# Linear attention with tokens on partitions: the divisor beside the sums, one reciprocal of 128x4, and quotients turned by TensorE

## The chip, the core and the metric
One NeuronCore of a Trainium2 chip runs the whole program in one launch. The metric is the device time of that launch in microseconds. Its engines are TensorE (PE in the profile; its weight loads are PEld), VectorE (DVE), ScalarE (ACT), GpSimd (POOL) and SyncE (SP, which here only issues DMAs). They run side by side and meet at semaphores. Matmuls read SBUF and write PSUM; PSUM has banks of 128 partitions by 512 fp32.

## The reference
All tensors are fp32. Input x is 2 x 1024 x 512. A block of causal linear attention (16 heads of 128, 4 heads of keys and values, so 4 query heads share one of each) is followed by a feed-forward block with 2-of-4 sparsity; both have a LayerNorm before and behind them and are added to x. What concerns us:

```python
q, k = rope(q), rope(k)                     # 128 per head
qf, kf = elu(q) + 1.0, elu(k) + 1.0
def step(carry, inp):                       # over 1024 tokens
    state = state + k_s[..., :, None] * v_s[..., None, :]
    z = z + k_s
    num = jnp.einsum('bhe,bhed->bhd', q_s, state)
    den = jnp.einsum('bhe,bhe->bh', q_s, z)[..., None] + 1e-06
    return ((state, z), num / den)
return out @ Wo.T                           # then layernorm, + x
# afterwards: h = silu(x @ w_gate) * (x @ w_up); of each 4 the 2 largest |h| stay; h @ w_down
```

## The kernel before
The scan is done in chunks of 128 tokens. Each operand of a matmul is split into a high part (fp32r) and a low part (the rest), and a product is three matmuls: high x high, low x high, high x low (the helper `three`, L450).

The attention is 64 slots: 8 units (2 batches by 4 key heads) of 8 chunks, one unit having 4 query heads. Function `slot_a(s)` exists once for each engine and issues what that engine does in slot s; the order in which these functions are written is the order of each engine's queue. Three chunks are in flight: slot s computes scores for chunk s, sums for chunk m = s - 1 and the output projection for chunk s - 2.

- Scores (L564): keys x queries of 4 heads, 128 x 512, into `bank_s`. The vector engine multiplies by the causal mask (L982), ScalarE rounds to `s_hi` (L773), GpSimd subtracts to get `s_lo` (L1159, helper `lo`).
- Sums (L536 to L542), features of v on partitions: the numerator of 4 heads, 128 x 512, in `psO`, from v and the scores and from the running state `st_hi`, `st_lo` and the queries. The divisor has a bank of its own, `psD`: ones x scores, and a state column of k's sum spread over 128 columns. It is the same on all 128 partitions. Both together are `bank_od`.
- State (L548 to L552): keys x values with a column of ones, 128 x 130, accumulated in `bank_st` over 7 chunks; ScalarE and the vector engine take it apart in two steps each (L760, L761, L975, L976).
- Quotient: ScalarE takes the logarithm of the divisor (L764) and exp of its negative (L769) as a first 1/d; the vector engine improves it with L991 and L997 and multiplies with the numerator in L1002. This reads `bank_od` until its end, and the next slot's sums wait for it (`dve_a`). ScalarE rounds the quotient to `a_hi` (L787), GpSimd makes `a_lo`.
- Output (L578): 12 matmuls of quotient by wout into `bank_y`, added into `y_acc` (L1013).

Among them each slot has a projection of queries for a later chunk (12 matmuls of 512 columns, `queries`), and every fourth slot one of keys, one of values, and turns of these and of x (4 transposes each, L497, L504, L476). In slots with odd s the vector engine starts with the rotation of the new queries (L913 to L922), which can begin when they are projected. Every job of normalisation (L887) waits for a small power step on GpSimd (L1166). In the feed-forward half (`slot_f`) all is projection and selection.

Of the kernel before, what the change touches and what calls it, by code (L numbers as in the profile page):

```python
# [7 lines left out]
ALU = mybir.AluOpType  # L8
ACT = mybir.ActivationFunctionType
# [156 lines left out]
def build(nc, x, wq, wk, wv, wo, wg, wu, wd, cos_t, sin_t, causal, eye, x1, out):  # L166
    with ExitStack() as ctx:
# [26 lines left out]
        Sth = sb("st_hi", [P, 2, P], F32R)  # L194
        Stl = sb("st_lo", [P, 2, P], F32R)
# [5 lines left out]
        small = sb("small", [P, 48])  # L201
# [11 lines left out]
        shift = [small[:, 40 + i:41 + i] for i in range(4)]  # L213

# [4 lines left out]
        rotk, xk, Ek, Sf, r0, Tn = [scr[:, i, :] for i in range(10, 16)]  # L219
# [42 lines left out]
        def sums(m):  # L262
            if m >= FREE and m % 2 == 0:
                return psQ[:, 0, :], psQ[:, 1, :]
            return psO, psD
# [40 lines left out]
        act_sth, act_ln, act_r0, act_sh, act_ah = [sem(n) for n in ("act_sth", "act_ln", "act_r0", "act_sh", "act_ah")]  # L306
# [3 lines left out]
        dve_T, dve_U, dve_a, dve_y = sem("dve_T"), sem("dve_U"), sem("dve_a"), sem("dve_y")  # L310
        pool_fl, pool_kl, pool_sl, pool_al = sem("pool_fl"), sem("pool_kl"), sem("pool_sl"), sem("pool_al")
# [135 lines left out]
        def _(pe):  # L447
# [67 lines left out]
            def slot_a(s):  # L515
# [4 lines left out]
                if 0 <= m < SLOTS:  # L520
# [3 lines left out]
                    psM, psN = sums(m)  # L524
                    o3 = psM.rearrange("p (h t) -> p h t", h=4)
                    d3 = psN.rearrange("p (h t) -> p h t", h=4)
                    qh, ql = big_h[:, p % 2, :, t], big_l[:, p % 2, :, t]
# [8 lines left out]
                    three(psM, Vh[:, c, 0:P], Vl[:, c, :], Sh[:, :], Sl[:, :], True, first)  # L536
                    pe.matmul(psN, ones[:, :], Sh[:, :], start=True, stop=False, skip_group_check=True)
                    ins = pe.matmul(psN, ones[:, :], Sl[:, :], start=False, stop=first, skip_group_check=True)
                    if not first:
                        g.wait_ge(dve_stl, 7 * u + ms)  # L540
                        three(o3, Sth[:, 0, :], Stl[:, 0, :], qh, ql, False, True)
                        ins = three(d3, Sth[:, 1, :], Stl[:, 1, :], qh, ql, False, True)  # L542
                    ins.then_inc(pe_pv, 1)
                    if ms < 7:
# [5 lines left out]
                        pe.matmul(psSt[:, 0:VP], KTl[:, c, :], Vh[:, c, :], start=False, stop=False,  # L550
                                  skip_group_check=True)
                        pe.matmul(psSt[:, 0:P], KTh[:, c, :], Vl[:, c, :], start=False, stop=True,  # L552
# [5 lines left out]
                if 0 <= s < SLOTS:  # L558
# [4 lines left out]
                    g.wait_ge(dve_s, s)  # L563
# [9 lines left out]
                if 0 <= m2 < SLOTS:  # L573
                    g.wait_ge(pool_al, m2 + 1)
# [4 lines left out]
                    ins.then_inc(pe_y, 1)  # L579

# [19 lines left out]
            def slot_f(n):  # L600
                tick = tick_f(n)
                if n < SLOTS:
# [7 lines left out]
                    if n > 0:  # L610
                        g.wait_ge(dve_s, SLOTS)
# [54 lines left out]
        def _(act):  # L666
# [77 lines left out]
            def slot_a(s):  # L744
# [11 lines left out]
                if 0 <= m < SLOTS:  # L756
                    u, ms = m // 8, m % 8
                    if ms < 7:
                        g.wait_ge(pe_st, 7 * u + ms + 1)
                        copy(Sth[:, 0, :], psSt[:, 0:P])  # L760
                        copy(Sth[:, 1, :], psSt[:, P:P + 1].to_broadcast([P, P])).then_inc(act_sth, 1)  # L761
                    g.wait_ge(pe_pv, m + 1)
                    g.wait_ge(dve_U, m)
                    act.activation(r0, sums(m)[1], ACT.Ln, bias=eps_den[:, 0:1]).then_inc(act_ln, 1)  # L764
                if s % 4 == 0 and 0 < s < SLOTS:
                    values_split(s // 4)
                if 0 <= m < SLOTS:
                    g.wait_ge(act_ln, m + 1)
                    act.activation(r0, r0, ACT.Exp, scale=-1.0).then_inc(act_r0, 1)  # L769
# [14 lines left out]
                if 0 <= m < SLOTS:  # L784
                    g.wait_ge(dve_a, m + 1)
# [76 lines left out]
        def _(dve):  # L862
# [94 lines left out]
            def slot_a(s):  # L957
# [56 lines left out]
                if s % 4 == 0 and 0 < s < SLOTS:  # L1014
                    turned_low(s // 4)
# [293 lines left out]
```

## Time and profile before

| | us |
|---|---|
| median of 3 runs | 1312.8 (1311.62 to 1313.56) |
| profiled execution, its own time | 1309.38 |
| its span | 1307.6 |
| PE busy | 1245.6 (95%) |
| DVE busy | 935.0 (72%) |
| POOL busy | 675.9 (52%) |
| ACT busy | 570.7 (44%) |

Times in the rows are microseconds from the span's start; the profiled execution took 1.8 us more than its span. An engine's busy time counts from the start of its instructions to their ends. TensorE's matmuls overlap, each starting before the one before has ended, so the rate is read from start to start. The attention takes the time up to about 757 us.

### The profile page before, as it was taken

The numbers are of one execution on the slowest core, as the hardware profiler recorded it, in microseconds if no ns is written. First come the engines' busy times: TensorE is split into PE (matmuls) and PEld (weight loads), VectorE is DVE, ScalarE is ACT, GpSimd is POOL, SyncE is SP. The second block draws the span as 40 slices with busy tenths as digits, with TensorE's granted clock in tenths as the row PEclk, the third lists the DMA queues.
The fourth block names the chain that finished last, engine by engine and source line by source line (L and its number), as shares of the span: only waits on it lengthen the run. The fifth ranks groups of instructions, "written<-read, shape, count | busy, mean of one in ns | idle before, by whom it ended". The sixth has DMA issues, their size and how long they took to land.

```text
span 1307.6 us, 15436 instructions
## 1 busy us (share of the span) xinstructions
PE 1245.6 (95%) x5543; PEld 1008.7 (77%) x5543; DVE 935.0 (72%) x1426; ACT 570.7 (44%) x1002; POOL 675.9 (52%) x524
## 2 busy tenths in 40 slices
PE   7889999999998899999998899999999999999996
PEld 7668778888787687787786677888888878888885
DVE  8678778878777777887867746666657775555568
ACT  4544654655554555546455433333333233332322
POOL 6365665565567756655646754343434644242414
PEclk9899999999999999999999999999999999999998
DMA  5321312211322312222212232222122321121103
GB/s 185 101 57 49 91 55 57 65 57 33 97 81 73 105 49 77 69 57 81 56 25 75 92 101 64 65 60 62 42 64 65 121 73 57 41 57 41 49 1 112
DMA packets 50347, 90.26 MB, mean 69 GB/s; under 512 B 6496, under 2 KB 6752, under 8 KB 50272
## 3 DMA queue, kind: packets, MB, share of 16 engines
q1 hardware_dynamic: 50272, 89.29, 23.1%
q8 instruction: 44, 0.72, 0.2%
q14 instruction: 31, 0.25, 0.1%
HBM read 64.09 MB, written 8.39 MB: 55 GB/s over the span
## 4 chain that ended last, share of the span: by engine, by line
PE 63%; DVE 17%; POOL 8%; ACT 5%; issue 4%; DMA 2%; SPq 1%; DVEq 0%; POOLq 0%
PE bank_q L451 6%; PE bank_q L453 6%; PE bank_q L452 6%; PE bank_od L451 6%; PE bank_od L453 6%; PE bank_od L452 6%; PE bank_t L451 3%; PE bank_t L452 3%; PE bank_t L453 3%; POOL s_lo L1159 3%; PE bank_s L451 3%; PE bank_s L453 3%; PE bank_s L452 3%; PE bank_y L451 2%; PE bank_y L453 2%
## 5 line engine op out<-in xcount | busy, mean ns | idle before, releaser
L1159 POOL TENSOR_TENSOR big_lo<-scratch,big_hi 128x1024 fp32r<-128x1024 f32 (+1 forms) x64 | 150.4, 2360 | 236.1 <-ACT big_hi L817 217.1
L1159 POOL TENSOR_TENSOR w_lo<-stage,w_hi 128x512 fp32r<-128x512 f32 x96 | 153.3, 1605 | 68.3 <-ACT w_hi L701 66.8
L451 PE MATMUL bank_q<-x_hi,w_hi 128*128 128x512 f32 x440 | 173.0, 393 | 1.3 <-DVE scratch L917 1.3
L453 PE MATMUL bank_q<-x_lo,w_hi 128*128 128x512 f32 x440 | 171.9, 391 | 0.0
L452 PE MATMUL bank_q<-x_hi,w_lo 128*128 128x512 f32 x440 | 171.6, 390 | 0.0
L1159 POOL TENSOR_TENSOR s_lo<-scratch,s_hi 128x512 fp32r<-128x512 f32 x64 | 94.5, 1477 | 140.7 <-ACT s_hi L773 140.7
L808 ACT ACTIVATE scratch<-scratch 128x512 f32<-128x512 f32 x64 | 40.5, 632 | 233.4 <-DVE scratch L1076 233.2
L1159 POOL TENSOR_TENSOR a_lo<-scratch,a_hi 128x512 fp32r<-128x512 f32 x64 | 82.9, 1295 | 97.2 <-ACT a_hi L787 97.2
L451 PE MATMUL bank_y<-wout_hi,a_hi 128*128 128x512 f32 x256 | 103.2, 403 | 6.1 <-POOL a_lo L1159 3.0
L787 ACT CAST a_hi<-scratch 128x512 fp32r<-128x512 f32 x64 | 39.7, 621 | 155.6 <-DVE scratch L1002 155.6
L1094 DVE TENSOR_TENSOR y_acc<-bank_od,y_acc 128x512 f32<-128x512 f32 x44 | 30.2, 686 | 101.5 <-PE bank_od L453 101.5
L453 PE MATMUL bank_y<-wout_lo,a_hi 128*128 128x512 f32 x256 | 101.3, 396 | 0.0
L452 PE MATMUL bank_y<-wout_hi,a_lo 128*128 128x512 f32 x256 | 101.3, 396 | 0.0
L451 PEld LDWEIGHTS bank_q<-x_hi,w_hi 128*128 128x128 f32 x440 | 82.8, 188 | 19.0 <-issue 1.7
L452 PEld LDWEIGHTS bank_q<-x_hi,w_lo 128*128 128x128 f32 x440 | 82.7, 188 | 17.6
L453 PEld LDWEIGHTS bank_q<-x_lo,w_hi 128*128 128x128 f32 x440 | 82.6, 188 | 17.7
L927 DVE SCALAR_TENSOR_TENSOR scratch<-scratch 128x1024 f32<-128x1024 f32 x31 | 42.9, 1383 | 48.6 <-ACT scratch L736 48.6
L451 PE MATMUL bank_t<-x_hi,w_hi 128*128 128x512 f32 x192 | 76.0, 396 | 1.6 <-DVE kt_lo L949 1.4
L817 ACT CAST big_hi<-scratch 128x512 fp32r<-128x512 f32 x64 | 39.2, 623 | 86.6 <-DVE scratch L1048 76.2
L452 PE MATMUL bank_t<-x_hi,w_lo 128*128 128x512 f32 x192 | 75.7, 394 | 0.0
L453 PE MATMUL bank_t<-x_lo,w_hi 128*128 128x512 f32 x192 | 75.6, 394 | 0.0
L773 ACT CAST s_hi<-scratch 128x512 fp32r<-128x512 f32 x64 | 39.8, 622 | 70.2 <-DVE scratch L982 70.2
(285 smaller groups left out, 3436.9 us busy)
## 6 DMA issues: line engine op xcount, KB each, us to landing
scratch<-scratch SPq DMA_DIRECT2D x124, 128.0 KB, 2.6
x_rows<-x SPq DMA_DIRECT2D x56, 256.0 KB, 2.9
stage<-wq SPq DMA_DIRECT2D x32, 256.0 KB, 2.7
stage<-wo SPq DMA_DIRECT2D x32, 256.0 KB, 2.6
stage<-wg SPq DMA_DIRECT2D x32, 256.0 KB, 2.7
stage<-wu SPq DMA_DIRECT2D x32, 256.0 KB, 2.6
stage<-wd SPq DMA_DIRECT2D x32, 256.0 KB, 2.6
x<-x_rows SPq DMA_DIRECT2D x16, 256.0 KB, 2.3
```

The lines of the kernel that those rows point to most:

```text
L451: pe.matmul(ps, whi, xhi, start=first, stop=False, skip_group_check=True)
L452: pe.matmul(ps, wlo, xhi, start=False, stop=False, skip_group_check=True)
L453: return pe.matmul(ps, whi, xlo, start=False, stop=last, skip_group_check=True)
L773: copy(Sh[:, :], Sf).then_inc(act_sh, 1)
L787: copy(Ah[:, :, :].rearrange("p h t -> p (h t)"), Tn).then_inc(act_ah, 1)
L808: act.activation(ab[:, i, :], hid[:, i, :], ACT.Abs).then_inc(act_ab, 1)
L817: copy(big_h[:, d % 2, i, :], hid[:, i, :]).then_inc(act_hh, 1)
L927: dve.scalar_tensor_tensor(whole, grown, 1.0, whole, ALU.min, ALU.add).then_inc(dve_f, 1)
L1094: dve.tensor_tensor(Y[:, t, :], down_bank(y), Y[:, t, :], ALU.add).then_inc(dve_yf, 1)
L1159: return pool.tensor_tensor(dst, full, hi.bitcast(F32), ALU.subtract)
```

## The change
The sums are formed with tokens on partitions. The scores of a head (128 x 128) are now the weights, and v with its column of ones (130 columns) is streamed; the same with queries and the state. So a head's sums are 130 columns wide, and column 128 is its divisor, one value for each token, which is a partition. Four heads lie in two banks (`sums(m)[:, h // 2, h % 2, :]`). The divisor's bank, the ones and the spread state column go. Division is then: 4 divisors out of PSUM with the offset, one reciprocal of 128 x 4, one multiplication with a broadcast operand, all on the vector engine. The output projection needs features on partitions, so TensorE turns the 4 quotients by transposes into `bank_s`, which the mask has read by then; ScalarE rounds from there, and the low part is made by the vector engine instead of GpSimd. The scores of the next chunk now wait for that low part (`dve_al`). The state is taken out in one step by each of ScalarE and the vector engine.

```diff
         def sums(m):
-            if m >= FREE and m % 2 == 0:
-                return psQ[:, 0, :], psQ[:, 1, :]
-            return psO, psD
+            both = psQ if m >= FREE and m % 2 == 0 else psOD
+            return both[:, :, 0:2 * VP].rearrange("p g (i d) -> p g i d", i=2)
...
@@ TensorE, slot_a
-                    three(psM, Vh[:, c, 0:P], Vl[:, c, :], Sh[:, :], Sl[:, :], True, first)
-                    pe.matmul(psN, ones[:, :], Sh[:, :], start=True, stop=False, skip_group_check=True)
-                    ins = pe.matmul(psN, ones[:, :], Sl[:, :], start=False, stop=first, skip_group_check=True)
                     if not first:
                         g.wait_ge(dve_stl, 7 * u + ms)
-                        three(o3, Sth[:, 0, :], Stl[:, 0, :], qh, ql, False, True)
-                        ins = three(d3, Sth[:, 1, :], Stl[:, 1, :], qh, ql, False, True)
+                    for h in range(4):
+                        o = sums(m)[:, h // 2, h % 2, :]
+                        sh, sl = Sh[:, h * P:(h + 1) * P], Sl[:, h * P:(h + 1) * P]
+                        qh, ql = big_h[:, p % 2, h, t], big_l[:, p % 2, h, t]
+                        pe.matmul(o, sh, Vh[:, c, :], start=True, stop=False, skip_group_check=True)
+                        pe.matmul(o[:, 0:P], sh, Vl[:, c, :], start=False, stop=False, skip_group_check=True)
+                        ins = pe.matmul(o, sl, Vh[:, c, :], start=False, stop=first, skip_group_check=True)
+                        if not first:
+                            pe.matmul(o, qh, Sth[:, :], start=False, stop=False, skip_group_check=True)
+                            pe.matmul(o, qh, Stl[:, :], start=False, stop=False, skip_group_check=True)
+                            ins = pe.matmul(o, ql, Sth[:, :], start=False, stop=True, skip_group_check=True)
...
                     g.wait_ge(pool_fl, 2 * p + 2)
-                    g.wait_ge(dve_s, s)
+                    g.wait_ge(dve_al, s - 1)
...
                 if 0 <= m2 < SLOTS:
-                    g.wait_ge(pool_al, m2 + 1)
+                    g.wait_ge(dve_al, m2 + 1)
...
+                if 0 <= m < SLOTS:
+                    g.wait_ge(dve_a, m + 1)
+                    g.wait_ge(dve_s, min(s + 1, SLOTS))
+                    for h in range(4):
+                        ins = pe.transpose(psS[:, h * P:(h + 1) * P], Tn[:, h * P:(h + 1) * P], ident[:, :])
+                    ins.then_inc(pe_at, 1)
@@ ScalarE, slot_a
                     if ms < 7:
+                        g.wait_ge(pe_pv, m)
                         g.wait_ge(pe_st, 7 * u + ms + 1)
-                        copy(Sth[:, 0, :], psSt[:, 0:P])
-                        copy(Sth[:, 1, :], psSt[:, P:P + 1].to_broadcast([P, P])).then_inc(act_sth, 1)
-                    g.wait_ge(pe_pv, m + 1)
-                    g.wait_ge(dve_U, m)
-                    act.activation(r0, sums(m)[1], ACT.Ln, bias=eps_den[:, 0:1]).then_inc(act_ln, 1)
+                        copy(Sth[:, :], psSt[:, 0:VP]).then_inc(act_sth, 1)
...
-                    act.activation(r0, r0, ACT.Exp, scale=-1.0).then_inc(act_r0, 1)
...
-                    g.wait_ge(dve_a, m + 1)
+                    g.wait_ge(pe_at, m + 1)
                     g.wait_ge(pe_y, m)
-                    copy(Ah[:, :, :].rearrange("p h t -> p (h t)"), Tn).then_inc(act_ah, 1)
+                    copy(Ah[:, :, :].rearrange("p h t -> p (h t)"), psS[:, :]).then_inc(act_ah, 1)
@@ VectorE, slot_a
-                    dve.scalar_tensor_tensor(Tn, sums(m)[1], EPS_DEN, r0, ALU.add, ALU.mult).then_inc(dve_T, 1)
+                    g.wait_ge(pe_pv, m + 1)
+                    dve.tensor_scalar(den.rearrange("p (g i o) -> p g i o", g=2, i=2), sums(m)[:, :, :, P:P + 1],
+                                      EPS_DEN, None, ALU.add).then_inc(dve_den, 1)
+                    g.wait_ge(dve_den, m + 1)
+                    dve.reciprocal(share, den).then_inc(dve_share, 1)
+                    g.wait_ge(dve_share, m + 1)
+                    g.wait_ge(pe_at, m)
+                    dve.tensor_tensor(Tn.rearrange("p (g i d) -> p g i d", g=2, i=2), sums(m)[:, :, :, 0:P],
+                                      share.rearrange("p (g i o) -> p g i o", g=2, i=2).to_broadcast([P, 2, 2, P]),
+                                      ALU.mult).then_inc(dve_a, 1)
...
-                    dve.scalar_tensor_tensor(Tn, Tn, 2.0, r0, ALU.subtract, ALU.mult).then_inc(dve_U, 1)
...
-                    dve.scalar_tensor_tensor(Tn, Tn, -1.0, sums(m)[0], ALU.mult, ALU.mult).then_inc(dve_a, 1)
...
+                if 0 <= m < SLOTS:
+                    g.wait_ge(act_ah, m + 1)
+                    g.wait_ge(pe_y, m)
+                    dve.tensor_tensor(Al[:, :, :].rearrange("p h t -> p (h t)"), psS[:, :],
+                                      Ah[:, :, :].rearrange("p h t -> p (h t)").bitcast(F32),
+                                      ALU.subtract).then_inc(dve_al, 1)
@@ GpSimd, slot_a
-                if 0 <= m < SLOTS:
-                    g.wait_ge(act_ah, m + 1)
-                    lo(Al[:, :, :].rearrange("p h t -> p (h t)"), Tn,
-                       Ah[:, :, :].rearrange("p h t -> p (h t)")).then_inc(pool_al, 1)
```

The vector engine's queue in slot s = 9 (m = 8, the first chunk of a unit), before, from the rotation's last step to the output's addition:

```order
L922 TENSOR_TENSOR scratch<-scratch 128x1024
L894 TENSOR_TENSOR x_lo<-bank_t,x_hi 128x4x128
L975 TENSOR_TENSOR st_lo<-bank_st,st_hi 128x128
L976 TENSOR_TENSOR st_lo<-bank_st,st_hi 128x128
L982 TENSOR_TENSOR scratch<-bank_s,mask 128x512
L991 SCALAR_TENSOR_TENSOR scratch<-bank_od,scratch 128x512
L997 SCALAR_TENSOR_TENSOR scratch<-scratch 128x512
L1002 SCALAR_TENSOR_TENSOR scratch<-scratch,bank_od 128x512
L1011 COPY y_acc<-bank_y 128x512
```

The same place in the changed kernel (its own line numbers):

```order
L926 TENSOR_TENSOR scratch<-scratch 128x1024
L898 TENSOR_TENSOR x_lo<-bank_t,x_hi 128x4x128
L979 TENSOR_TENSOR st_lo<-bank_st,st_hi 128x130
L985 TENSOR_TENSOR scratch<-bank_s,mask 128x512
L993 TENSOR_SCALAR small<-bank_od 128x4
L996 RECIPROCAL small<-small 128x4
L999 TENSOR_TENSOR scratch<-bank_od,small 128x512
L1015 COPY y_acc<-bank_y 128x512
L1021 TENSOR_TENSOR a_lo<-bank_s,a_hi 128x512
```

The product (L999) stands right behind the two small steps, ahead of any normalising step of the slot, and the low part of the quotients is new at the end.

TensorE's queue in the same slot of the changed kernel, from the last head's sums to the next projection of queries; before, 5 matmuls of 512 columns stood for the 12 small ones and nothing stood between the output and the queries:

```order
L539 MATMUL bank_od<-v_hi,s_hi 128x130
L540 MATMUL bank_od<-v_lo,s_hi 128x128
L541 MATMUL bank_od<-v_hi,s_lo 128x130
L551 MATMUL bank_st<-v_hi,kt_hi 128x130
L553 MATMUL bank_st<-v_lo,kt_hi 128x128
L555 MATMUL bank_st<-v_hi,kt_lo 128x130
L452 MATMUL bank_s<-big_hi,k_hi 128x512
L453 MATMUL bank_s<-big_hi,k_lo 128x512
L454 MATMUL bank_s<-big_lo,k_hi 128x512
...
L454 MATMUL bank_y<-wout_lo,a_hi 128x512
L588 MATMUL bank_s<-ident,scratch 128x128 x4
L452 MATMUL bank_q<-x_hi,w_hi 128x512
```

The transposes (L588) come between the output and the queries, so whatever they wait for, the projections behind them wait for too.

## Rows read from the trace of the kernel before

**Rows 1.** The page: busy time of each engine, share of the span, instructions.

```profile
PE 1245.6 (95%) x5543; PEld 1008.7 (77%) x5543; DVE 935.0 (72%) x1426; ACT 570.7 (44%) x1002; POOL 675.9 (52%) x524
```

**Rows 2.** Busy us by stretch: PE, PEld, DVE, ACT, POOL, granted clock, DMA.

```profile
64.00:696.00 632.00, 605.80 (x2733) 488.12 (x2733) 493.62 (x705) 338.09 (x600) 379.22 (x266) 0.99 0.23 65
696.00:757.00 61.00, 49.95 (x213) 36.79 (x213) 44.55 (x72) 29.56 (x58) 41.84 (x38) 1.00 0.26 81
...
406.30:409.70 3.40, 3.28 (x8) 2.63 (x9) 2.29 (x4) 3.03 (x4) 1.57 (x2) 0.50 0.05 18
```

**Rows 3.** Waits of TensorE: us in total, times, longest us.

```profile
PE bank_od L451 <- DVE scratch L1002: 21.1, 16, 3.1
...
PE bank_od L451 <- POOL s_lo L1159: 5.4, 4, 2.4
...
PE bank_q L451 <- POOL s_lo L1159: 2.5, 3, 1.1
```

**Rows 4.** Timeline of TensorE, slot m = 8: start us, duration us, what.

```profile
148.99 0.40 PE L538 MATMUL bank_od<-s_lo,ones 128*128 128x512 f32 x1
149.23 0.22 PE L548 MATMUL bank_st<-v_hi,kt_hi 128*128 128x130 f32 x1
149.29 0.28 PE L550 MATMUL bank_st<-v_hi,kt_lo 128*128 128x130 f32 x1
149.40 0.27 PE L552 MATMUL bank_st<-v_lo,kt_hi 128*128 128x128 f32 x1
149.51 0.45 PE L451 MATMUL bank_s<-big_hi,k_hi 128*128 128x512 f32 x1
149.80 0.40 PE L452 MATMUL bank_s<-big_hi,k_lo 128*128 128x512 f32 x1
```

**Rows 5.** Timeline of TensorE, four transposes of values.

```profile
410.54 0.60 PE L497 MATMUL bank_t<-ident,scratch 128*128 128x128 f32 x4
410.90 0.47 PE L451 MATMUL bank_s<-big_hi,k_hi 128*128 128x512 f32 x1
411.21 0.39 PE L452 MATMUL bank_s<-big_hi,k_lo 128*128 128x512 f32 x1
```

**Rows 6.** Timeline, slot m = 8: the vector engine's chain, TensorE's first query matmul.

```profile
147.65 1.22 DVE L913 TENSOR_TENSOR scratch<-bank_q,scratch 128x1024 f32<-128x1024 f32 x1
...
150.10 2.28 DVE L922 TENSOR_TENSOR scratch<-scratch 128x1024 f32<-128x1024 f32 x1
...
153.30 0.67 DVE L982 TENSOR_TENSOR scratch<-bank_s,mask 128x512 f32<-128x512 f32 x1
...
153.06 0.39 PE L451 MATMUL bank_q<-x_hi,w_hi 128*128 128x512 f32 x1
```

**Rows 7.** Groups of instructions: busy us, mean ns; one line: ns min/median/max.

```profile
L975 DVE TENSOR_TENSOR st_lo<-bank_st,st_hi 128x128 fp32r<-128x128 f32 x56 | 15.8, 282 | 6.8 <-ACT st_hi L761 6.6
...
L881 DVE BATCH_NORM_AGGREGATE small<-small 128x2 f32<-128x6 f32 x64 | 11.6, 182 | 2.2
...
L1159 POOL TENSOR_TENSOR a_lo<-scratch,a_hi 128x512 fp32r<-128x512 f32 x64 | 82.9, 1295 | 97.2 <-ACT a_hi L787 97.2
...
L922 DVE TENSOR_TENSOR scratch<-scratch x31: 1249/1957/2525, 29.0 to 691.0; 128x1024 f32<-128x1024 f32 x31
```

**Rows 8.** Timeline of the first slots: mask of m = 0, sums of m = 1.

```profile
66.88 0.67 DVE L982 TENSOR_TENSOR scratch<-bank_s,mask 128x512 f32<-128x512 f32 x1
...
70.06 0.50 PE L451 MATMUL bank_od<-s_hi,v_hi 128*128 128x512 f32 x1 [2.41 <-POOL s_lo L1159]
```

**Rows 9.** Timeline of ScalarE: the logarithms of m = 58 and m = 62.

```profile
712.70 0.71 ACT L764 ACTIVATE scratch<-bank_q,small 128x512 f32<-128x512 f32 x1
...
747.59 0.70 ACT L764 ACTIVATE scratch<-bank_q,small 128x512 f32<-128x512 f32 x1
```

**Rows 10.** Timeline of TensorE at the start: streams of 128-column matmuls.

```profile
2.67 5.38 PE L639 MATMUL bank_t<-ones 128*128 128x128 f32 x24 [2.67 <-DVE v_hi L1112]
...
11.89 1.53 PE L639 MATMUL bank_t<-ones 128*128 128x128 f32 x12
```

**Rows 11.** Weight loads of line 538: busy us, mean ns.

```profile
L538 PEld LDWEIGHTS bank_od<-s_lo,ones 128*128 128x128 f32 x61 | 11.9, 195 | 2.9
```

More of the change, by code:

```diff
@@ L193, in build @@
         Al = sb("a_lo", [P, 4, P], F32R)
-        Sth = sb("st_hi", [P, 2, P], F32R)
-        Stl = sb("st_lo", [P, 2, P], F32R)
+        Sth = sb("st_hi", [P, VP], F32R)
+        Stl = sb("st_lo", [P, VP], F32R)
         ones = sb("ones", [P, P], F32R)
@@ L200, in build @@
         xr = sb("x_rows", [P, RING_R, W])
-        small = sb("small", [P, 48])
+        small = sb("small", [P, 52])
         Wh = [w_hi[:, i, :] for i in range(6)] + [Kh[:, :], Sh[:, :]]
@@ L213, in build @@
         shift = [small[:, 40 + i:41 + i] for i in range(4)]
+        den, share = small[:, 44:48], small[:, 48:52]
         M1, M2, xq = scr[:, 0:2, :], scr[:, 2:4, :], scr[:, 4:6, :]
@@ L218, in build @@
         sinb = scr[:, 8:10, :]
-        rotk, xk, Ek, Sf, r0, Tn = [scr[:, i, :] for i in range(10, 16)]
+        rotk, xk, Ek, Sf, zero, Tn = [scr[:, i, :] for i in range(10, 16)]
         vT = rotk
@@ L305, in build @@
         act_qe, act_qh = sem("act_qe"), sem("act_qh")
-        act_sth, act_ln, act_r0, act_sh, act_ah = [sem(n) for n in ("act_sth", "act_ln", "act_r0", "act_sh", "act_ah")]
+        pe_at = sem("pe_at")
+        act_sth, act_sh, act_ah = sem("act_sth"), sem("act_sh"), sem("act_ah")
         dve_q, dve_x, dve_f = sem("dve_q"), sem("dve_x"), sem("dve_f")
@@ L309, in build @@
         dve_stl, dve_s, dve_vl, dve_ktl = sem("dve_stl"), sem("dve_s"), sem("dve_vl"), sem("dve_ktl")
-        dve_T, dve_U, dve_a, dve_y = sem("dve_T"), sem("dve_U"), sem("dve_a"), sem("dve_y")
-        pool_fl, pool_kl, pool_sl, pool_al = sem("pool_fl"), sem("pool_kl"), sem("pool_sl"), sem("pool_al")
+        dve_den, dve_share, dve_a, dve_al, dve_y = [sem(n) for n in ("dve_den", "dve_share", "dve_a", "dve_al", "dve_y")]
+        pool_fl, pool_kl, pool_sl = sem("pool_fl"), sem("pool_kl"), sem("pool_sl")
         pe_g, pe_u, pe_d = sem("pe_g"), sem("pe_u"), sem("pe_d")
@@ L523, in slot_a @@
                     first = ms == 0
[L524 to L527, printed above, removed]
                     g.wait_ge(pool_sl, m + 1)
@@ L549, in slot_a @@
                                   skip_group_check=True)
-                        pe.matmul(psSt[:, 0:VP], KTl[:, c, :], Vh[:, c, :], start=False, stop=False,
+                        pe.matmul(psSt[:, 0:P], KTh[:, c, :], Vl[:, c, :], start=False, stop=False,
                                   skip_group_check=True)
-                        pe.matmul(psSt[:, 0:P], KTh[:, c, :], Vl[:, c, :], start=False, stop=True,
+                        pe.matmul(psSt[:, 0:VP], KTl[:, c, :], Vh[:, c, :], start=False, stop=True,
                                   skip_group_check=True).then_inc(pe_st, 1)
@@ L610, in slot_f @@
                     if n > 0:
-                        g.wait_ge(dve_s, SLOTS)
+                        g.wait_ge(dve_al, SLOTS)
                     project(psG[n % 2], j, half).then_inc(pe_g, 1)
@@ L974, in slot_a @@
                     g.wait_ge(act_sth, i + 1)
[L975 to L977 removed]
+                    dve.tensor_tensor(Stl[:, :], psSt[:, 0:VP], Sth[:, :].bitcast(F32),
+                                      ALU.subtract).then_inc(dve_stl, 1)
                 if 0 <= s < SLOTS:
@@ L1107, in _ @@
             dve.memset(Sf, 1.0).then_inc(dve_const, 1)
-            dve.memset(r0, 0.0).then_inc(dve_const, 1)
+            dve.memset(zero, 0.0).then_inc(dve_const, 1)
             g.wait_ge(dve_const, 2)
@@ L1112, in _ @@
             dve.tensor_copy(Vh[:, :, P + 1:P + 2],
[L1113 removed]
+                            zero[:, 0:4].rearrange("p (c o) -> p c o", o=1)).then_inc(const_ok, 1)
             variance(FIRST[0])
```

12 lines of the change are left out of this document (removed).

## The prediction, on record before the change was run

> **What bounds the kernel now.** I read the busy shares first [rows 1]: the reader is to see TensorE at 95% and no other engine above 72%. Then the two stretches of the attention half [rows 2]: in 64 to 696 us TensorE is busy for 606 of 632 us, in its last 61 us only for 50; the feed-forward half behind them (757 to 1307 us, 550 us) is not touched by the change. Third, who TensorE waits for [rows 3]: nearly all of it stands before the first matmul of the sums, for the last vector step of the slot before (L1002) or for s_lo from GpSimd. So the change pays in two currencies: what TensorE has to issue per slot, and what it waits for in a slot. A slot is one pass of slot_a, 64 of them; m is the slot whose sums are formed, 8 slots make a unit, and "first" slots are those with m a multiple of 8.
>
> Busy times of matmuls overlap, so I count start to start. A 512-column matmul takes 0.23 us (148.99 to 149.23), one of 128 or 130 columns with its own weights 0.11 (149.29, 149.40, 149.51), and the step from the small ones back to wide ones costs 0.06 more in the second wide one (149.51 to 149.80 is 0.29) and is given back by the short first one (149.23 to 149.29) [rows 4]. Four transposes and what follows: 410.54 to 410.90, then 0.31 instead of 0.23, together 0.44 us [rows 5].
>
> **Sums and state on TensorE: +8.1 us.** In an ordinary slot, 11 wide matmuls and 3 small ones now take 11 x 0.233 + 0.34 = 2.90 us; afterwards 24 + 3 small ones take 27 x 0.112 = 3.02. That is +0.12 in 56 slots, 6.7 us. In the 8 first slots 5 wide ones (and 3 small) become 12 small ones: 15 x 0.112 = 1.68 for 1.50, +1.4 us. Moving 512 columns as four times 128 saves no time here, because each piece brings its own weight load; the saving of the change is that the divisor rides along.
>
> The trace has 0.11 us for a small matmul with its load. The Trainium skill ("TensorE: Matmul & The Clock Gate", section "Back-to-back issue gap") gives about 81 ns for such a pair of 128 columns in a stream; by it, 1720 new small matmuls would cost 53 us less. The trace does not agree in either place where it has such pairs, and the same page's load time of columns over 1.2 (107 ns for 128, section "LDWEIGHTS") fits the rows.
>
> **Transposes: +28.2 us.** 64 x 0.44 us; nothing covers them, they stand on the engine that bounds.
>
> **What TensorE no longer waits for.** The sums of a slot wait for L1002 because it reads their banks, and L1002 stands behind a logarithm, an exponential, two more vector steps and the normalising step, which itself waits for GpSimd. Afterwards the banks are free one short chain after the mask: offset, reciprocal, product. The 16 waits for L1002 are 21.1 us in the view; it counts from the modelled end of the matmul before, 0.17 us after the next could start (0.40 long, 0.23 pitch), so they are 23.8. The 7 waits for s_lo are 7.9 + 1.2 = 9.1 [rows 3]. The first of these (2.6, at 70.06 [rows 8]) and the 5.5 us of the last slots are counted below. Left are 24.8 us, and I take all of them as gone: s_lo follows the mask by 2 us, the wait for the product comes sooner and stops TensorE first. With them goes 0.08 us of exposed weight load in 16 places, 1.3 us, and some 1 us of waits for wout_lo, whose queue on GpSimd gets shorter. Four of the waits were followed by a clock of 1.2 GHz for 3.4 us (granted 0.50, the last of the four is in rows 2), at most 1.7 us lost in each, in sum 6.3 us by the pitch of 0.43 there. Sum: -33.4 us.
>
> **The last slots: -10 us.** Without projections of queries TensorE needs some 6.55 us a slot, but the logarithms of m = 58 and 62 start at 712.70 and 747.59 [rows 9], 8.7 us a slot. They are held by the ring mask, s_hi, s_lo (1.3 to 1.7 us, behind a_lo, w_lo and an addition), deviation, normalise, L1002, a_hi, a_lo. The change takes a_lo from GpSimd and the normalising step out of the way of the banks. After the mask's end at M I get s_lo at M+2.0, the deviation at M+3.3, normalise M+3.9, Y added M+4.5, the new low part M+5.2, and the next scores want it at about M+5.5. So TensorE bounds, at 7.1 us a slot: 4 x 2.2 idle us go, and 1.7 at the last Y; 0.5 stays.
>
> **The wait that is added: +9.8 us.** The transposes need the product, which needs the mask, and queued behind them on TensorE are the queries, keys and values, and so everything. The vector engine's new chain after the mask is two small steps and one of 512. Neither small step is in the trace. Nearest is the aggregate on 6 columns, 0.18 us; above it a 128-column step from PSUM, 0.28 [rows 7]; below, nothing. I take 0.18 each (the widths are 4), 0.04 between dependent steps, 0.68 for the product (the mask has the same shape and a broadcast operand), together 1.13 us. At 0.28 each the late slots add 5 us, at nothing they give back 6.
> Slot m = 8 shows it [rows 6]. Rotation starts at 147.65, when the queries end; the mask ends at 153.97, the product would at 155.1; but Y has ended by 153.06, 2.0 us before. What helps: L922 took 2.28 there because GpSimd ran big_lo beside it (the line's fastest is 1.25 [rows 7]), and with a_lo gone big_lo runs earlier; one small step less before the mask (0.2). TensorE takes 0.2 more. That leaves 0.9 us. It holds for the first slots, whose sums are short: 8 x 0.9. Slot m = 32 has a variance before its rotation and I give it 2.1. In the others rotation or the keys' turn also end late now (mask 2.3 us late in m = 9 and its like), but from the transposes of the slot before, TensorE needs 12.0 us (24 projections at 0.23 and 6.5 for the rest), as the key projection lies between, and I read some 11 for the other engines. In m = 3, 7, ... the mask comes at once and 0.1 to 0.3 us is left. For these together 1.5 us.
>
> **The start: +3.0 us.** In m = 0 the mask starts at 66.88 [rows 8], so the transposes at 68.8; the queries that ran before it now follow, and the next sums begin near 71.8 instead of 70.06: +1.7. TensorE then stands for 5 us, and I put 1.3 us of slow clock behind it.
>
> **Covered, at nothing.** ScalarE loses the logarithm, the exponential and half of st_hi, GpSimd 1.3 us a slot [rows 7], and the vector engine three steps of 512 and a small one for the product, the low part of 0.68 and the two small ones, about 1 us net; all were idle for 20% or more. The low part on the vector engine stands behind normalise, but the next scores that wait for it come 6 us after the transposes. If that cover goes it costs what normalise is late; the longest wait for L1002 was 3.1 us [rows 3].
>
> **Sum.** 8.1 + 28.2 - 33.4 - 10 + 9.8 + 3.0 = +5.7 us on the profiled execution's 1309.4 (span 1307.6): 1315.1. The median of the runs lies 3.4 higher, so 1318.5.
>
> **Rivals.**
> - The wait at the transposes does not come, and neither do its slots' others: DVE and GpSimd gain so much that product and Y always meet. Then 9.8 and the start's 3.0 fall away: 1306, faster by 7. For it speaks that GpSimd's load falls by 12% (82.9 of 675.9 us) [rows 1, 7] and L922 varies from 1.25 to 2.5 with it; against it the 2.0 us of m = 8, a chain whose start TensorE itself sets.
> - The wait comes in full. The comparison of m = 8 made for all slots, with the engines as they run now, leaves 50 us of shortfall instead of 9.8, of which the 8 first slots have 16 and m = 9, 17, ... as much. Some 24 us of it would come back as work of the others overlapping: 1318.5 + 16 to 40, middle 1343. For it: the vector engine is 78% busy here [rows 2] and TensorE has given its slack away in the middle of the slot; against: after a stall it starts its next chain relatively earlier.
> - Small matmuls run at 0.081 us. As said above, 1720 x 0.031 = 53 us less, 1265. Both groups of rows speak against it.
> - The load is left out where two matmuls in a row have the same weights (2 of 6 in a head, 1 of 3 in the state). Each would save half of 0.112: 9 of them in 56 slots and 5 in 8, 544 x 0.056 = 30 us less, 1288. Against it: L538 loads the ones again right behind L537 [rows 11].
> - The clock. With 31 small steps in a slot TensorE might be given 1.2 GHz once per slot; a slow stretch costs 1.7 us [rows 2], 64 of them 109 us, 1427. Against it: at the start the pitch halved, from 0.22 to about 0.11, in a stream of nothing but 128-column matmuls and transposes [rows 10]. The Trainium skill (same page, "PE-mode transpose") says that transposes do not count as activity; by that, this rival is likelier than I have it, but the four that the trace has in every fourth slot have brought no fall.
>
> **How the numbers follow.** Forecast 0.52, own range 1310 to 1328 (the unknown small steps 11 us wide, the start and the last slots 3 each); no wait 0.24; wait in full 0.15; the last three 0.03 each. A change within 0.2% (2.6 us) can't be told from none. Faster: nearly all of the second case, the fourth and third, and a little of the first, 0.28. Same 0.17, from the low part of the first and the top of the second. Slower 0.55. The range goes from 1300 to 1342: below it lie the two cases of cheap matmuls, above it the clock and the upper half of the wait in full.
>
> **What the profile after would show.** Right: small matmuls at 0.11 pitch; no wait for the product before the sums; waits of TensorE before the transposes, on the vector engine, about 1 us in the first slots; TensorE's instruction count up, 64 x 4 transposes at 0.44; the last slots 7 us apart; few stretches at 0.50. Wrong: waits before the transposes in most slots, or before the scores for the low part; an offset or reciprocal well over 0.2 us; a pitch under 0.1; a clock that falls in each slot.

## The result, and the profile after

| | median us | runs | profiled execution us | span us | granted clock |
|---|---|---|---|---|---|
| before | 1311.5 | 20 (1309.31 to 1315.15) | 1309.38 | 1307.6 | 0.989 |
| changed | 1313.85 | 20 (1312.74 to 1314.91) | 1313.69 | 1311.9 | 0.991 |

The changed kernel is slower by 2.35 us, ratio 1.0016 [1.0009, 1.0022]: the direction of the forecast (+5.7 us, to 1318.5), less than half its size, and under the 0.2% that I had set as the bound of "no change". Note that the two profiled executions are 4.3 us apart and the medians 2.35. One run of the kernel before, in the chip's slow state (1528 us at a granted clock of 0.753), is left out of every figure here.

The page of the changed kernel, busy time of each engine:

```profile
PE 1271.0 (97%) x6583; PEld 1072.6 (82%) x6583; DVE 889.3 (68%) x1434; ACT 486.7 (37%) x818; POOL 561.4 (43%) x460
```

Against [rows 1] TensorE issues 1040 matmuls more; every other engine got lighter, GpSimd by 114 us. Still the time rose: what TensorE has to issue counted for more.

The same stretches as [rows 2]; the last two rows are the two stretches with a slow clock behind the first transposes and in slot m = 32:

```profile
64.00:696.00 632.00, 620.22 (x3587) 535.14 (x3588) 448.54 (x700) 260.35 (x431) 272.98 (x208) 0.99 0.24 64
696.00:757.00 61.00, 58.05 (x365) 50.44 (x362) 40.46 (x77) 23.08 (x43) 33.21 (x31) 1.00 0.31 91
...
67.50:73.90 6.40, 5.47 (x15) 4.50 (x16) 2.32 (x5) 2.28 (x4) 1.47 (x2) 0.50 0.62 164
432.60:435.40 2.80, 2.80 (x8) 2.21 (x7) 1.74 (x3) 1.67 (x3) 0.57 (x2) 0.50 0.82 229
```

TensorE's 26 idle us in the long stretch are 12 now, its 11 idle us in the last are 3. The waits of TensorE, to be read beside [rows 3] (us in total, times, longest):

```profile
PE bank_s L588 <- DVE scratch L999: 14.3, 11, 4.8
PE bank_s L477 <- DVE x_lo L898: 6.5, 1, 6.5
PE bank_od L452 <- DVE y_acc L1104: 2.7, 1, 2.7
```

The 29.0 us of waits for L1002 and s_lo are gone without a rest. A new wait stands at the transposes (L588) for the product (L999): 4.8 us in m = 0, the remaining ten together 9.5. The other two rows are not of the change.

TensorE in slot m = 8, small matmuls and then the step to wide ones (compare [rows 4]):

```profile
152.71 0.27 PE L539 MATMUL bank_od<-v_hi,s_hi 128*128 128x130 f32 x1
152.82 0.27 PE L540 MATMUL bank_od<-v_lo,s_hi 128*128 128x128 f32 x1
152.93 0.28 PE L541 MATMUL bank_od<-v_hi,s_lo 128*128 128x130 f32 x1
153.04 0.28 PE L551 MATMUL bank_st<-v_hi,kt_hi 128*128 128x130 f32 x1
...
156.69 0.40 PE L454 MATMUL bank_y<-wout_lo,a_hi 128*128 128x512 f32 x1
157.66 0.66 PE L588 MATMUL bank_s<-ident,scratch 128*128 128x128 f32 x4 [0.56 <-DVE scratch L999]
158.07 0.48 PE L452 MATMUL bank_q<-x_hi,w_hi 128*128 128x512 f32 x1
```

The pitch (the step from one start to the next) is 0.11 us. From 152.71 (L539) to 152.82 (L540) the weights are the same, s_hi, and the step is 0.11 like any other: no load is left out. From the last matmul of Y (the output projection) to the transposes it is 0.97, so 0.74 of waiting. The vector engine in front of it (compare [rows 6]):

```profile
153.97 1.23 DVE L926 TENSOR_TENSOR scratch<-scratch 128x1024 f32<-128x1024 f32 x1
...
155.92 0.68 DVE L985 TENSOR_TENSOR scratch<-bank_s,mask 128x512 f32<-128x512 f32 x1
156.52 0.15 DVE L993 TENSOR_SCALAR small<-bank_od 128x4 f32<-128x4 f32 x1
156.70 0.18 DVE L996 RECIPROCAL small<-small 128x4 f32<-128x4 f32 x1
156.91 0.69 DVE L999 TENSOR_TENSOR scratch<-bank_od,small 128x512 f32<-128x512 f32 x1
```

From the mask's end to the product's end is 1.00 us; 1.13 had been forecast.

Groups of instructions (busy us, mean ns; for [rows 7]):

```profile
L1021 DVE TENSOR_TENSOR a_lo<-bank_s,a_hi 128x512 fp32r<-128x512 f32 x64 | 43.8, 684 | 14.8 <-ACT a_hi L791 14.8
...
L999 DVE TENSOR_TENSOR scratch<-bank_od,small 128x512 f32<-128x512 f32 x61 | 42.2, 691 | 2.3 <-DVE small L996 0.3
...
L926 DVE TENSOR_TENSOR scratch<-scratch 128x1024 f32<-128x1024 f32 x31 | 39.8, 1284 | 1.1
...
L996 DVE RECIPROCAL small<-small 128x4 f32<-128x4 f32 x64 | 11.4, 178 | 2.2
L993 DVE TENSOR_SCALAR small<-bank_od 128x4 f32<-128x4 f32 x61 | 9.1, 150 | 0.0
```

**A budget of TensorE.** For each kernel I split the time from the first instruction to the first down-projection matmul by the steps from one matmul's start to the next. A step up to 0.26 us is issue. Of a longer one 0.23 is issue, and what is over that is put down by the step's length to an exposed load (up to 0.38; a weight load that the matmul before did not cover), to the slow clock (up to 0.45) or to a wait (beyond). The bounds are mine: a small matmul at half clock, 0.22 us, still counts as issue.

| us | end | waits | slow clock | exposed | issue |
|---|---|---|---|---|---|
| before | 794.2 | 52.8 | 8.3 | 11.8 | 721.2 |
| changed | 798.2 | 26.6 | 4.5 | 10.2 | 757.0 |
| measured | +4.0 | -26.2 | -3.8 | -1.6 | +35.8 |
| forecast | +5.7 | -24.3 | -5.0 | -1.3 | +36.3 |

So the change is a trade of 36 us of issue for 26 of waits and 5 of slow clock and loads; each column came out within 2 us of its forecast (the parts are rounded).

### The profile page after: what moved, and what is told of

Read it like the earlier page. It is cut to its first block, busy times and chain, and to the rows that moved or that the text cites. A ratio compares the mean times of both kernels' runs of the same rounds, so it can differ in the third digit from the quotient of the medians.

```text
span 1311.9 us, 17285 instructions
## 1 busy us (share of the span) xinstructions
PE 1271.0 (97%) x6583; PEld 1072.6 (82%) x6583; DVE 889.3 (68%) x1434; ACT 486.7 (37%) x818; POOL 561.4 (43%) x460
## 3 DMA queue, kind: packets, MB, share of 16 engines
q1 hardware_dynamic: 50272, 89.29, 24.5%
## 4 chain that ended last, share of the span: by engine, by line
PE 84%; DVE 11%; issue 2%; ACT 1%; POOL 1%; DMA 1%; SPq 0%; DVEq 0%
PE bank_q L452 8%; PE bank_q L454 8%; PE bank_q L453 8%; PE bank_t L454 4%; PE bank_t L452 4%; PE bank_t L453 4%; PE bank_od L452 4%; PE bank_od L454 4%; PE bank_od L453 4%; PE bank_y L454 4%; PE bank_y L452 4%; PE bank_y L453 4%; PE bank_s L452 3%; PE bank_s L454 3%; PE bank_s L453 3%; PE bank_s L588 2%
## 5 line engine op out<-in xcount | busy, mean ns | idle before, releaser
L1169 POOL TENSOR_TENSOR s_lo<-scratch,s_hi 128x512 fp32r<-128x512 f32 x64 | 83.4, 1303 | 317.5 <-ACT s_hi L777 317.5
L452 PE MATMUL bank_q<-x_hi,w_hi 128*128 128x512 f32 x440 | 178.8, 406 | 0.0
L1169 POOL TENSOR_TENSOR w_lo<-stage,w_hi 128x512 fp32r<-128x512 f32 x96 | 141.2, 1480 | 81.1 <-ACT w_hi L711 80.2
L541 PE MATMUL bank_od<-v_hi,s_lo 128*128 128x130 f32 x244 | 67.4, 276 | 0.0
L540 PE MATMUL bank_od<-v_lo,s_hi 128*128 128x128 f32 x244 | 66.8, 274 | 0.0
L539 PE MATMUL bank_od<-v_hi,s_hi 128*128 128x130 f32 x244 | 65.0, 266 | 0.0
```

Source lines behind the costliest of these rows:

```text
L452: pe.matmul(ps, whi, xhi, start=first, stop=False, skip_group_check=True)
L539: pe.matmul(o, sh, Vh[:, c, :], start=True, stop=False, skip_group_check=True)
L540: pe.matmul(o[:, 0:P], sh, Vl[:, c, :], start=False, stop=False, skip_group_check=True)
L541: ins = pe.matmul(o, sl, Vh[:, c, :], start=False, stop=first, skip_group_check=True)
L1169: return pool.tensor_tensor(dst, full, hi.bitcast(F32), ALU.subtract)
```

## The experiments

**1. The kernel before once more, unchanged.**

> The kernel before, unchanged, to see how its own time varies. Theory (clock): the profile of before (1309.4) had four falls of the clock after waits of 2.2 to 3.5 us; which waits are followed by a fall differs from run to run, so runs with a lower mean granted clock are longer by about 1.7 us per fall, and the median of many runs lies near 1311.5 with a mean clock of 0.988 or less. Rival (offset): time outside the span or something else than TensorE's clock makes the difference; then the runs show no relation between time and clock.

Measured: 1311.54 us (11 runs, 1309.8 to 1312.98), ratio 0.9997 [0.9988, 1.0006]; its profiled execution was at 1310.24. What each run shows beside its time is its mean granted clock. For 38 runs of the kernel before it is recorded (these 11, 17 that ran beside the first experiments and 10 beside the later ones):

| granted clock | runs | mean us |
|---|---|---|
| 0.987, 0.988 | 12 | 1310.4 |
| 0.985, 0.986 | 22 | 1311.9 |
| 0.983 | 4 | 1313.2 |

The profiled execution of before, at 0.989 and 1309.38, is faster than all 38 (one of the 20 runs in the first table, 1309.31, matches it): it was a draw from the fast edge of a wide scatter. The changed kernel's 20 runs are all at 0.989 to 0.991, and its profiled one (1313.69) is 0.2 below its median; in experiments 2 to 8 the profile lies between 0.3 below and 1.5 above the median. So 2.1 us of the distance between profile and median belong to the kernel before alone. The rival of time outside the span is ruled out: each recorded run is 1.75 to 1.87 us above its span. That the lower clock comes from more falls behind its waits fits: [rows 2] shows one, and this experiment's own profile (0.988, 0.9 us longer) has six stretches at half clock before 757 us (23.9 us in all) where before's has five (20.5). Runs of one clock still differ by up to 2.6 us, and no execution at 0.985 or 0.983 was profiled.

**2. The kernel before with the product ahead of the normalising step.** This takes from the change only where L1002 stands. In the cuts of code, round brackets stand for lines that are not printed.

```
+                if 0 <= m < SLOTS:
+                    (wait for dve_U; the product, -> dve_a)
                 for job in at(tick, norm_tick, LATER):
                     normalise(job)
-                if 0 <= m < SLOTS:
-                    (wait for dve_U; the product, -> dve_a)
```

> The kernel before with one edit: the quotient's last step (L1002) stands ahead of the normalising step instead of behind it. Theory: the 24 us that TensorE waited for L1002 came mostly from the normalising step in between, which itself waits for GpSimd; with it go most of those waits and the clock falls behind them: TensorE's waits for L1002 fall from 21.1 to under 6 us, and the time by 18 to 26 us, to 1286 to 1294, with no change to the layout of the sums. Rival: the chain of logarithm, exponential and two steps is late by itself, and the next wait (s_lo) is right behind: then 5 to 10 us, 1301 to 1307.

Measured: 1282.64 us (4 runs, 1281.11 to 1283.76), ratio 0.9778 [0.9765, 0.9792], 29 us less than before. Its waits of TensorE:

```profile
PE bank_od L451 <- POOL s_lo L1159: 6.5, 6, 2.4
PE bank_s L476 <- DVE x_lo L894: 6.5, 1, 6.5
PE bank_t L476 <- DVE kt_lo L949: 3.2, 3, 1.1
...
PE bank_od L451 <- DVE scratch L1000: 0.8, 1, 0.8
```

Of the 16 waits for the product (here L1000) one of 0.8 us is left, and s_lo's before the sums comes to 6.5 us. The budget has waits 20.8 us lower, slow clock 4.8, exposed loads 1.3, issue as before (721.5). Their sum is about the 26.6 us between the two profiled executions; the 2.3 left of the 28.9 are about what before's usual run lies above its profile (2.1, experiment 1). This is 27 of the 32 us that the change wins, at none of its price; experiment 6 has the rest.

**3. The changed kernel with the transposes behind the queries** (in slots whose number is no multiple of 4).

```
+                if 0 <= m < SLOTS and s % 4 == 0:
+                    turn_quotients()
                 if s % 4 == 0 and 0 < s < SLOTS:
                     turn_keys(s // 4)
...
                 if s + 7 < SLOTS:
                     queries(s + 7)
+                if 0 <= m < SLOTS and s % 4:
+                    turn_quotients()
```

> The changed kernel, with the transposes of the quotients moved behind the projection of queries (in slots with s not a multiple of 4; elsewhere they stay). Theory: the 16 us that TensorE waited at the transposes (5.0 of it in the first slot) come from their place alone; outside the last slots, which have no projection of queries, about 9 us of them go, 1.5 of the first slot's 5.0 and some 3.5 us of slow clock: 1298 to 1301. Rival: the low part, on the vector engine, then comes later, holds up the rotation behind it, and TensorE waits as long at the scores or at the transposes of the next slot: within 3 us of 1313.9.

Measured: 1307.55 us (8 runs, 1306.67 to 1309.57), ratio to before 0.9972 [0.9961, 0.9982], 6.3 us less than the changed kernel. Waits fell from 26.6 to 19.3 us, and the view shows where the rest went:

```profile
PE bank_s L588 <- DVE scratch L1004: 4.1, 4, 2.2
...
PE bank_st L551 <- DVE kt_lo L958: 1.3, 1, 1.3
PE bank_s L452 <- DVE a_lo L1026: 1.2, 1, 1.2
...
PE bank_q L452 <- DVE scratch L926: 1.1, 1, 1.1
```

The time lies between the theory's range and the rival's, in neither. The wait at the transposes is now 4.1 instead of 14.3, other waits have come up to 1.3, 1.2 and 1.1 (the first from 0.4, the others from nothing), and the slow clock stayed (5.1 us in the budget, 4.5 before the edit). So the theory holds for the place, not for its whole price: this move is worth 6 us.

**4. Each group of transposes issued twice.**

```
-                    for h in range(4):
+                    for h in (0, 1, 2, 3) * 2:
```

> The changed kernel with each group of four transposes issued twice, into the same place. Theory (TensorE bounds, the transposes are bare): 4 x 0.109 us more in 64 slots, 27.9 us, less 1 to 3 us where TensorE waited anyway and the others catch up: 1338 to 1342. Rival (TensorE has slack behind its waits): half of it or less, under 1328.

Measured: 1338.14 us (4 runs, 1337.91 to 1339.49), ratio 1.0204 [1.019, 1.0218], 24.3 us more than the changed kernel; in the budget issue +27.0, waits -2.2. 27.0 over 64 is 0.42 us a group, as the theory had it: the transposes' price is real and nothing covers it.

**5. The changed kernel with the product behind the keys' sum and the normalising step**, the order of the kernel before.

```
                     dve.reciprocal(share, den).then_inc(dve_share, 1)
-                    (the product, -> dve_a)
                 for p in range(1, STEPS): ... key_sum(p)
                 for job in at(tick, norm_tick, LATER):
                     normalise(job)
+                if 0 <= m < SLOTS:
+                    (the product, -> dve_a)
```

> The changed kernel with the product put back to where the kernel before had its last step: behind the keys' sum and the normalising step. Theory (the gain of the change is the product's place, not the cheaper division): TensorE now waits for the product at the transposes, with nothing of its own in between; the normalising step stands there in some 50 slots and itself comes 3 us or more after the mask, so the waits at the transposes grow from 16 to 60 us or more: 1350 to 1380. Rival (the short division is what counts): the chain without logarithm and exponential is early enough, and at most 10 us are added, under 1325.

Measured: 1473.64 us (4 runs, 1470.68 to 1475.13), ratio 1.1233 [1.1216, 1.1251]: 160 us more than the changed kernel. Its wait at the transposes and its long stretch:

```profile
PE bank_s L588 <- DVE scratch L1005: 112.8, 41, 5.2
```

```profile
64.00:696.00 632.00, 546.91 (x2924) 463.54 (x2923) 368.22 (x578) 214.40 (x355) 224.06 (x175) 0.92 0.21 54
```

The direction was expected, the size was not (1350 to 1380). 41 slots wait, and TensorE's clock stood at half in 33 stretches, 171 us in all (4 and 25 in the changed kernel); the budget has waits +110, slow clock +38. In the old layout the same order costs 34 us of time (experiment 6 against the kernel before). There the sums that wait come a whole query projection later; here the transposes come right behind Y, and everything else is queued behind them. A part of the size looks like a loop: the rotation's first step waits for the queries, which now stand behind late transposes, and mask and product come behind the rotation. Its idle time before, in the changed kernel and then in this one:

```profile
L917 DVE TENSOR_TENSOR scratch<-bank_q,scratch 128x1024 f32<-128x1024 f32 x31 | 37.9, 1223 | 19.3 <-PE bank_q L454 19.2
...
L917 DVE TENSOR_TENSOR scratch<-bank_q,scratch 128x1024 f32<-128x1024 f32 x31 | 38.0, 1224 | 49.9 <-PE bank_q L454 49.8
```

That this order of queues is the reason is read from the code and these rows; no run moved the transposes with the product late.

**6. The product ahead of the keys' sum too** (experiment 2 with one step more moved).

```
+                (deviation; product)
                 for p in range(1, STEPS): ... key_sum(p)
-                (deviation)
                 for job in at(tick, norm_tick, LATER):
```

> The kernel before with its product ahead of the normalising step (1282.6) and now ahead of the keys' sum too, which waits 1.1 us for ScalarE in the slots of a new block of keys. Theory: the vector engine's chain in 15 slots gets 1 to 2 us shorter, but TensorE's waits for the product are gone already, so only the next steps behind move: 1280 to 1283. Rival: the keys' sum is late for the keys' turn or high part then, and 1284 or more.

Measured: 1277.4 us (4 runs, 1276.28 to 1280.23), ratio 0.9743 [0.9728, 0.9758], 34 us less than before and 36 less than the changed kernel. The expectation (1280 to 1283) was missed by 2.6 us. The budget has waits 27.2, where experiment 2 has 32.0, and slow clock 2.6; of experiment 2's view the waits for kt_lo before the turns of x (3.2 us) and for the product (0.8) are gone. It is the fastest of all, with the old layout. Against the kernel before, waits, slow clock and exposed loads are 32.7 us lower, and in the changed kernel 31.6: with the vector order of the change the old layout has all of its gain.

**7. Experiment 2, and the low part a_lo on the vector engine instead of GpSimd.**

```
+                if 0 <= m < SLOTS:      # vector engine, behind Y
+                    dve.tensor_tensor(Al..., Tn, Ah..., ALU.subtract).then_inc(dve_al, 1)
...
-                    lo(Al..., Tn, Ah...).then_inc(pool_al, 1)      # GpSimd
```

> The kernel before with its product early (1282.6), and the low part of the quotients on the vector engine instead of GpSimd: one part of the change alone. Theory: GpSimd's relief of 1.3 us a slot shortens its queue and the steps beside it on the vector engine (L922 1.77 towards 1.3 us), and the last slots, held by GpSimd's ring, come down from 8.7 to 7 us: 1272 to 1277. Rival: the vector engine, at 81% in this version, gets 0.7 us a slot more and a wait for ScalarE, and becomes the bound: 1284 or more.

The deviation (L991 before) then waits for `a_hi` too, which costs it nothing in the trace. Measured: 1307.17 us (5 runs, 1306.89 to 1308.13), ratio 0.9969 [0.9956, 0.9981]: 24.5 us worse than experiment 2. The rival was right. Stretch, waits and groups:

```profile
64.00:696.00 632.00, 600.01 (x2724) 484.66 (x2725) 551.43 (x760) 340.85 (x600) 300.28 (x209) 0.99 0.24 64
```

```profile
PE bank_od L451 <- POOL s_lo L1166: 11.5, 10, 2.4
PE bank_t L476 <- DVE kt_lo L949: 8.8, 8, 1.4
...
PE bank_t L497 <- DVE x_lo L894: 6.0, 8, 1.0
PE bank_st L548 <- DVE kt_lo L949: 5.7, 3, 3.1
```

```profile
L1018 DVE TENSOR_TENSOR a_lo<-scratch,a_hi 128x512 fp32r<-128x512 f32 x64 | 66.6, 1041 | 3.6 <-ACT a_hi L787 0.7
...
L922 DVE TENSOR_TENSOR scratch<-scratch 128x1024 f32<-128x1024 f32 x31 | 39.8, 1285 | 1.1
```

The vector engine is busy for 551 of 632 us (510 in experiment 2), and TensorE now waits for its other steps (kt_lo, x_lo) and longer for s_lo: in the budget the waits are 54.5 us, 22.5 more than in experiment 2. L922 did get fast, 1285 ns, but that did not pay.

**8. Experiments 6 and 7 together.**

> Both edits of the two kernels before this one in the list, on the kernel before with its early product. Theory: they touch different waits, and what each gives adds up within 2 us. Rival: with the low part on the vector engine its queue is the bound, and the keys' sum in either place makes no difference.

Measured: 1307.8 us (6 runs, 1306.59 to 1309.33), ratio 0.9971 [0.9959, 0.9984]. The rival was right again: with the low part on the vector engine the place of the keys' sum makes no difference (1307.17 without), where it gave 5 us with the low part on GpSimd.

## Why the prediction was right in kind and too large

**The step that failed** is the last of the sum: "The median of the runs lies 3.4 higher, so 1318.5." I carried the distance between the profiled execution and the median of three runs of the kernel before over to the changed kernel. Of these 3.4 us, 1.3 were the small sample (1312.8 over three runs, 1311.5 over twenty), and 2.1 were particular to the kernel before, whose usual run is at a granted clock of 0.985 or 0.986 and not the profile's 0.989 (experiment 1). The changed kernel's profile and median are 0.2 apart. Had I added nothing, 1315.1 would have stood against 1313.85; I had removed "6.3 us" of slow clock from a profiled execution that had less of it than the usual one, and not asked whether the usual one would gain more. On the profiled executions themselves the sum said +5.7 and +4.3 was measured. So of the 3.35 us by which the change itself was overestimated (+5.7 against +2.35), 1.95 are this step and 1.4 are in the terms of the sum, whose larger misses partly cancelled: the waits that went were 4.2 us more than forecast, the new ones and the slow clock at the start about 3.5 more, issue and loads 0.8 less. That the sum came within 1.4 is to that extent luck. Why the usual run of before has the lower clock is not shown beyond experiment 1.

**Sums and state, transposes: right.** Forecast +36.3, measured +35.8 of issue. Pitch 0.11, no load left out, transposes 0.42 to 0.44; the rivals of cheap matmuls, of a load left out and of a clock that falls in each slot are ruled out by the trace (granted clock 0.99). The new small matmuls are 1440 and the transposes 256, 1696 in all, not the 1720 of the prediction. The Trainium skill ("TensorE: Matmul & The Clock Gate", "Back-to-back issue gap") gives about 81 ns for a pair of 128 columns; the trace does not agree, 109 to 114 ns in over a thousand new ones. As for the clock, 64 more groups of four transposes among other matmuls brought no fall by themselves: both falls shown above stand behind a wait of over 2 us (4.8 and 2.1 in the trace), and a third wait of 2.2 us, at 717.5, was followed by none. The Trainium skill (the same page, "PE-mode transpose") says that a transpose does not count as PE-busy in the same way; here that made no visible difference.

**What is no longer waited for: right, and too small.** All waits for L1002 and s_lo went. By the budget 42.6 us of waits went (26.2 net and 16.4 of new ones at the transposes); the forecast's terms come to 38.4, the last slots included. Experiments 2 and 6 add what I had not seen: this gain can be had by the place of the product on the vector engine alone, with the old, dearer division. Moved alone it is worth 29 us, with the keys' sum 34. I had written that the chain gets short, and taken the order for a part of it.

**The last slots: right.** The rounding to s_hi in the last slots (ScalarE):

```profile
725.44 0.62 ACT L777 CAST s_hi<-scratch 128x512 fp32r<-128x512 f32 x1 [1.20 <-DVE scratch L985]
732.81 0.62 ACT L777 CAST s_hi<-scratch 128x512 fp32r<-128x512 f32 x1 [0.84 <-DVE scratch L985]
740.22 0.62 ACT L777 CAST s_hi<-scratch 128x512 fp32r<-128x512 f32 x1 [1.20 <-DVE scratch L985]
747.17 0.62 ACT L777 CAST s_hi<-scratch 128x512 fp32r<-128x512 f32 x1 [1.21 <-DVE scratch L985]
```

7.0 to 7.4 us apart; 7.1 was forecast, 8.7 it had been.

**The added wait: place right, nearly right in size.** Forecast 9.8, measured start to start 11.3 in 11 slots: m = 8, 16, 24, 40, 48, 56 with 0.6 to 0.7 each (forecast 0.9), m = 32 with 2.2 (2.1), four others 5.0, one of them 2.4 in the last slots (1.5 for all of these). The forecast's 9.8 counts m = 0 once more, which the start has too; without it these 11 slots were put at 9.0, so the four others are where it was short. The rival "no wait" is ruled out. So is "in full": of its 50 us of shortfall 16.4 came, and of the 16 us in the first slots 11.3, of which 5.0 in m = 0. (Its middle, 1343, is a slip too: 1318.5 and 16 to 40 has its middle at 1346.5.) Experiment 5 shows how near it lay: one to three vector steps more ahead of the product and 41 slots wait.

**The start: too small.** Forecast +3.0, measured +4.2: TensorE at m = 0 and 1,

```profile
63.20 0.40 PE L454 MATMUL bank_s<-big_lo,k_hi 128*128 128x512 f32 x1
68.43 1.11 PE L588 MATMUL bank_s<-ident,scratch 128*128 128x128 f32 x4 [4.83 <-DVE scratch L999]
69.20 0.77 PE L452 MATMUL bank_q<-x_hi,w_hi 128*128 128x512 f32 x1
69.77 0.63 PE L453 MATMUL bank_q<-x_hi,w_lo 128*128 128x512 f32 x1
...
74.03 0.40 PE L454 MATMUL bank_q<-x_lo,w_hi 128*128 128x512 f32 x1
74.27 0.22 PE L539 MATMUL bank_od<-v_hi,s_hi 128*128 128x130 f32 x1
```

The sums of m = 1 begin at 74.27, 70.06 before. Behind the wait of 4.8 us the clock stood at 0.50 and the pitch at 0.43 until 74.03: eleven projection matmuls at 0.2 us extra and 0.3 for the transposes, 2.5 us where I had put 1.3.

**Covered work: right in the changed kernel, by a margin I did not see.** No matmul there waits for a_lo. Experiment 7 shows that the low part on the vector engine costs the old layout 24.5 us. There the vector engine is busy for 551 us in the long stretch against 449. Over the whole kernel its three steps of 512 for deviation and product take 85 us more than the product and the two small steps that replace them (150 against 65, with the three that read the other bank), and the low part itself takes 66.6 us, read from SBUF, against 43.8, read from PSUM. So mostly the steps that the cheap division takes away make room for the low part, and its source helps.

What stays open: what an execution of before at 0.985 looks like inside, and whether the transposes could go behind the queries without the other waits that came (experiment 3). The changed kernel with a_lo left on GpSimd was not tried.

## What to carry to other kernels

When a change brings a gain and a price together, try the part that could be had alone: here the place of one vector instruction was worth 29 to 34 us, and the new layout around it cost 36. A wait is cheap or dear by what is queued behind the instruction that waits: the same vector order cost 34 us ahead of sums and 160 ahead of transposes. And compare profile with profile and median with median: an offset between the two belongs to a kernel with its waits, and goes when they go.

## What the runs showed of the hardware

- GpSimd's work slows the vector engine's where both read SBUF. a_lo read from SBUF on the vector engine took 673 to 1555 ns (mean 1041, experiment 7); read from PSUM in the changed kernel, 672 to 694 ns in all 64. Instruction by instruction: of the first, the 28 beside which GpSimd was busy for under half of their time took 673 to 694 ns, the other 36 a mean of 1318; of the second, the 26 with GpSimd busy for 95% or more took 673 to 692. The Trainium skill ("SBUF — State Buffer", "Who interferes with whom") says that a vector instruction with two SBUF inputs contends with a GpSimd instruction that reads SBUF, and one with at most one such input, outside the modes that use two ports, does not; the two groups agree.
- The load moved rather than vanished: the rotation's sum (L922, now L926) fell from a mean of 1938 to 1284 ns, but the normalising step of x_rows rose from 911 to 1580 (1534 in experiment 7). It took over the place beside GpSimd's work: of the 56 normalising steps 3 ran with GpSimd busy for 95% of their time or more before and 16 now (1218 to 2552 ns), while the 22 with GpSimd idle for as much take 535 to 548. The group of x_rows in the changed kernel:

```profile
L891 DVE TENSOR_SCALAR x_rows<-x_rows,small 128x512 f32<-128x512 f32 x24 | 37.9, 1580 | 27.0 <-POOL small L1176 27.0
```

- A vector instruction on 4 columns takes 150 ns from PSUM (offset) and 178 as a reciprocal in SBUF, a low part of 128 columns from PSUM 282 [rows 7], one of 512 columns 684: even on 4 columns over half of the 128-column time remains.
